# Layer 1's, the pre-attention's and layer 2 routing's steps reordered; the recurrence's weights loaded in layer 0's block; an unread matmul a turn ahead of the attention

## The chip, the core and the metric

One core of a Trainium2 chip runs the whole program in one launch. The metric is the device time of one execution in microseconds (us). The core has five engines that run beside each other and meet only at semaphores: TensorE (PE: matmuls, and PEld: the loading of its stationary operand), VectorE (DVE), ScalarE (ACT), GpSimd (POOL) and SyncE (SP, which issues DMA transfers).

## The reference

The input is x, 64 batches of 128 tokens of 128 features, with an adjacency matrix of 128x128 for each batch. Four layers follow, each a graph part and a feed-forward part, both added to x after a layer norm. Cut to what matters here:

```
x = x + L0_gnn(norm(x), adj)    # relu(adj @ h @ W_rel + h @ W_root), h a second norm of x
x = x + L0_ffn(norm(x))         # recurrence over the 128 tokens: three gates, cell, hidden state; weights U_c U_i U_o V_c V_i V_o, biases b_c b_i b_o
x = x + L1_gnn(norm(x), adj)    # relu((adj @ (x @ W_bot)) / rowsum(adj) + x @ W_top + bias)
x = x + L1_ffn(norm(x))         # router on the mean over the tokens of each batch, top 2 of 8 experts for each batch
x = x + L2_gnn(norm(x), adj)    # attention, 8 heads of 16, softmax times the adjacency
x = x + L2_ffn(norm(x))         # shared expert (128 to 512 to 128) plus top 2 of 8 experts for each token
x = x + L3_gnn(norm(x), adj)
x = x + L3_ffn(norm(x))         # top 1 of 32 experts for each token
```

All of it is in 32-bit floats.

## The kernel before

The 64 batches are taken as 16 groups (NG) of 4 (G), so that a group is a tile of 128 partitions x 512 columns (GW). X, AT (the transposed adjacency), FEAT, AUX and EXP are large buffers in SBUF that the stages use in turn; `PS[0]` to `PS[7]` are the eight banks of PSUM. The program is a row of blocks. In a block each engine has its own instruction stream. Between two blocks all engines meet (`release`, line 97), and the semaphores are cleared.

The order of each stream is written out by hand. `in_turn` and `unrolled` (lines 56 and 65) take a list of pairs (lag, step): in turn j each step is issued for group j - lag, in the order of the list. An engine executes its stream in that order, so a step that waits holds back all steps behind it. `reused(engine, semaphore, i, lag)` (line 70) waits until step i - lag has given its buffer free; with lag 1 a single buffer is shared, with lag 2 there are two that alternate (`par` is i % 2).

The blocks that the change touches:

- Layer 0's graph part (lines 224 to 382). SP loads x and adj for 16 groups (lines 230, 231), two groups ahead, and has nothing else to do.
- The recurrence (from line 385). SP loads the nine weights and three tensors for layer 1 (lines 391 to 396). TensorE and ScalarE wait for the first nine. Each of 128 steps goes through TensorE, ScalarE and VectorE; unread matmuls (line 429) fill TensorE's pauses.
- Layer 1's graph part (lines 477 to 635). TensorE's turn is xT, hidden, project, root, feat, aggregate. `hidden` (line 603) transposes the recurrence's states of group j into PS[0], and VectorE's `add` (line 553) adds them to X and takes the statistics of the sum (lines 172 and 176). GpSimd makes the norm's factors from these (lines 509 to 513). ScalarE normalises (`norm`, line 573), TensorE transposes (`xT`, line 195), ScalarE copies (line 567), TensorE multiplies by the two weights (`project` line 615, `root` line 621) and by the adjacency (`aggregate`, line 633), VectorE adds the root part's bias (`root`, line 531), mixes (`mix`, line 539), adds and takes statistics (`add2`), ScalarE normalises again (`norm2`, line 581), TensorE transposes (`feat`, line 195), and ScalarE copies the result to FEAT, with the sum over each batch's tokens as a by-product of four activations (line 593, `accum_out`). That sum, XM, feeds layer 1's router.
- The pre-attention (lines 894 to 959). VectorE: statistics (`stats`) and the bias of the attention's output (`bias`, line 920). GpSimd: the factors. ScalarE: `norm` (line 931), the copies `xT` (line 937) and `values` (line 941). TensorE: `xT` and `values` (line 955, eight passes).
- Layer 2's routing (lines 1171 to 1447). Each token gets its two experts and a place in a list. GpSimd takes the deviation of group i (`dev`, lines 182 and 184) and sends the rows of group i to DRAM with eight indirect DMAs (`send`, line 1199). VectorE: `stats`, `norm` (line 1388), `top` (lines 1395 to 1404), `choice` (to line 1424), `place` (lines 1429 to 1436), `add` (line 1440). TensorE: `xT` (line 1252), `logits` (line 1259), `rank` (lines 1287 to 1293), and the shared expert's two products, `up` (line 1268, four matmuls of 512 columns) and `down` (line 1276). ScalarE: `xT`, `twin` (a second copy of the rows), `th`, `gelu` (line 1353). Then a table is made from the counts (line 1301 on), and the experts' part follows.

A matmul of 32-bit floats takes two passes, each a record of its own; a transpose takes one.

Of the kernel before, what the change touches and what calls it, by code (L numbers as in the profile page):

```python
# [78 lines left out]
def program(nc, a, out):  # L79
    ctx = ExitStack()  # L80
    with ctx:
# [74 lines left out]
        def column(v):  # L156
            return v.rearrange("(p a) -> p a", a=1)
# [58 lines left out]
        s = sems("l0", "in0 in1 adjT_ps adjT raw mv var pw rstd r2 xn x1 h_ps hT hw_ps hw conv relu back x2 "  # L216
# [6 lines left out]

        with nc.Block() as block:
            @block.sync
            def _(sp):
# [5 lines left out]
                unrolled(NG, [(0, load)])  # L232

# [137 lines left out]
        s = sems("rnn", "zero x_even x_odd g i o gt it ot hc ig c ct h w w1")  # L371
        wr = {}
        for gate in "cio":
            for mat in "UV":
                wr[mat + gate] = lb(f"w_{mat}{gate}", [H, H])
            wr["b" + gate] = lb(f"w_b{gate}", [H, 1])
# [7 lines left out]
        wtop, wbot = EXP[:, 4096:4096 + H], EXP[:, 4096 + H:4096 + 2 * H]  # L384
        b1rows = EXP[:, 4096 + 2 * H:4096 + 3 * H]
        ROWSUM = PS[6][:, 0:B]
        with nc.Block() as block:
            @block.sync
            def _(sp):
                for gate in "cio":  # L390
                    sp.dma_start(wr["U" + gate][:], a["L0_ffn_U_" + gate]).then_inc(s.w, 16)
                    sp.dma_start(wr["V" + gate][:], a["L0_ffn_V_" + gate]).then_inc(s.w, 16)
                    sp.dma_start(wr["b" + gate][:], column(a["L0_ffn_b_" + gate])).then_inc(s.w, 16)
                sp.dma_start(wtop, a["L1_gnn_weight"][0:H, :]).then_inc(s.w1, 16)
                sp.dma_start(wbot, a["L1_gnn_weight"][H:2 * H, :]).then_inc(s.w1, 16)
                sp.dma_start(b1rows, a["L1_gnn_bias"].partition_broadcast(P)).then_inc(s.w1, 16)
                sp.wait_ge(s.w1, 3 * 16)

# [6 lines left out]
            def _(pe):  # L405
                half = STEPS * B // 2

                def inputs(j, par, gate_at, part):

                    gate = "ico"[gate_at]  # L410
                    pe.matmul(PS[2 * gate_at + par][:, part * half:(part + 1) * half], wr["U" + gate][:],
# [3 lines left out]
                def turn(j, par, prefetch):  # L415

                    for u in range(STEPS):
                        step = j * STEPS + u
                        pe.wait_ge(s.h if step else s.zero, step if step else 2)
                        for gate_at, (gate, sem) in enumerate(zip("ico", (s.i, s.g, s.o))):  # L420
                            pe.matmul(PS[2 * gate_at + par][:, u * B:(u + 1) * B], wr["V" + gate][:],  # L421
# [8 lines left out]
                pe.wait_ge(s.w, 9 * 16)  # L430
# [7 lines left out]
            def _(act):  # L438
                def turn(j, par):
                    for u in range(STEPS):  # L440
                        step, sp_ = j * STEPS + u, u % 2
                        for at, (gate, made, done, f) in enumerate((("i", s.i, s.it, ACT.Sigmoid), ("c", s.g, s.gt, ACT.Tanh),
# [3 lines left out]
                                           bias=wr["b" + gate][:]).then_inc(done, 1)  # L446
# [46 lines left out]
        with nc.Block() as block:  # L493
# [1551 lines left out]
```

## Time and profile before

| | us |
|---|---|
| median of three runs | 2015.53 |
| the three runs | 2016.48, 1934.81, 2015.53 |
| the profiled execution, its own time | 1941.87 |
| its span, from the first to the last instruction | 1940.1 |

In the profiled execution the stretches between the meetings of all engines are: layer 0's graph part 0 to 110, the recurrence 110 to 413, layer 1's graph part 413 to 563, its router 563 to 585, its experts 585 to 725, the pre-attention 725 to 786, the attention 786 to 1054, layer 2's routing 1054 to 1261 and its table to 1272, its experts to 1540, layer 3 to the end.

How to read it: times are microseconds from the start of the span. PE is TensorE's matmuls, PEld its weight loads, SPq the queue of SyncE that issues DMAs. L553 is line 553 of the kernel. x8 behind a row says that eight instructions are merged in it. The clock is the granted clock of TensorE, 1.0 for 2.4 GHz and 0.5 for 1.2 GHz, in the mean over a stretch.

### The profile page before, as it was taken

Reading aid. Unit: us, or ns where it says so; the run is one execution under the profiler, and the core shown is the slowest. Engines: PE = TensorE matmul, PEld = TensorE weight load, DVE = VectorE, ACT = ScalarE, POOL = GpSimd, SP = SyncE. Lnnn points to the kernel's source line nnn. Section 1 sums busy time; section 2 is a strip of 40 time slices with the busy share of each in tenths; the row PEclk is TensorE's granted clock in tenths of the full one; section 3 lists DMA queues with packets and bytes.
Section 4 is the critical chain, followed back from the end, with each engine's and each line's share of the span. In section 5 each row is a group of like instructions: output and inputs, shape, how many; then the busy total and the mean of one; then the engine's idle time right before and its main releaser. Section 6 shows DMA issues by size and latency. Waiting matters only on the chain. (4 is left out here: it accounts for less than half of the span.)

```text
span 1940.1 us, 42716 instructions
## 1 busy us (share of the span) xinstructions
PE 1656.8 (85%) x13042; PEld 1362.5 (70%) x13042; DVE 1085.2 (56%) x4176; ACT 951.0 (49%) x2955; POOL 794.2 (41%) x1359
## 2 busy tenths in 40 slices
PE   7968899985649987899997799989999798884995
PEld 5746677765649986788885567789999655563663
DVE  7823333346546775699997645143333377743452
ACT  5844444436556656766664233356666444430000
POOL 6600000013326766111112577736656425543664
PEclk9989999988879995999998589989999899976886
DMA  3200000010004420000002211122222342105331
GB/s 112 66 13 2 1 1 1 1 25 1 1 20 130 125 85 1 2 3 2 3 3 71 81 48 50 52 65 71 71 73 71 87 114 72 48 29 107 92 86 32
DMA packets 129697, 92.87 MB, mean 48 GB/s; under 512 B 25166, under 2 KB 120305, under 8 KB 129476
## 3 DMA queue, kind: packets, MB, share of 16 engines
q1 hardware_dynamic: 108276, 61.46, 11.8%
q0 software_dynamic: 13568, 25.90, 4.1%
q10 hardware_dynamic: 7632, 2.79, 0.8%
q8 instruction: 112, 1.84, 0.4%
q14 instruction: 109, 0.89, 0.2%
HBM read 58.81 MB, written 33.35 MB: 48 GB/s over the span
## 5 line engine op out<-in xcount | busy, mean ns | idle before, releaser
L1207 POOL DMA_INDIRECT scratch_made<-FEAT x136 | 154.6, 1137 | 121.9 <-DVE FEAT L1496 119.1
L1365 ACT ACTIVATE FEAT<-BANKS,EXP 128x128 f32<-128x128 f32 x544 | 155.0, 368 | 82.7 <-PE BANKS L1318 82.7
L1060 ACT ACTIVATE EXP<-BANKS,NEGMAX 128x128 f32<-128x128 f32 x512 | 139.0, 382 | 59.3 <-DVE NEGMAX L1072 58.0
L1318 PE MATMUL BANKS<-FEAT 128*128 128x128 f32 x1088 | 145.4, 277 | 0.0
L1327 PE MATMUL BANKS<-AUX,FEAT 128*128 x1088 | 144.2, 276 | 0.4 <-ACT FEAT L1365 0.4
L1199 POOL DMA_INDIRECT scratch_sent<-FEAT,POS x128 | 123.7, 967 | 38.9 <-issue 37.8
L1318 PEld LDWEIGHTS BANKS<-FEAT 128*128 128x128 f32 x1088 | 133.9, 194 | 0.0
L1327 PEld LDWEIGHTS BANKS<-AUX,FEAT 128*128 128x128 f32 x1088 | 132.9, 193 | 0.6 <-issue 0.6
L509 POOL TENSOR_SCALAR NEG<-MV 128x4 f32<-128x4 f32 x16 | 3.6, 228 | 310.4 <-DVE MV L176 310.4
L989 POOL COPY EXP<-AUX 128x32 f32<-128x32 f32 x256 | 42.1, 209 | 215.8 <-PE BANKS L1035 215.8
L429 PE MATMUL BANKS<-FEAT,ident 128*128 128x256 f32 x460 | 126.8, 393 | 0.0
L1625 POOL DMA_INDIRECT out_x<-FEAT x96 | 93.9, 979 | 74.5 <-DVE FEAT L2012 46.6
L1496 DVE TENSOR_TENSOR FEAT<-BANKS,B2BC 128x128 f32<-128x128 f32 x136 | 39.5, 290 | 136.8 <-PE BANKS L1327 136.8
L464 DVE TENSOR_TENSOR ig<-gates 128x64 f32<-128x64 f32 x128 | 28.7, 224 | 119.0 <-ACT gates L445 119.0
L445 ACT ACTIVATE gates<-BANKS,w_bi 128x64 f32<-128x64 f32 x128 | 40.3, 315 | 108.7 <-PE BANKS L421 108.7
L1844 ACT ACTIVATE FEAT<-BANKS,EXP 128x128 f32<-128x128 f32 x24 | 8.8, 367 | 172.8 <-PE BANKS L1787 172.8
L1072 DVE TENSOR_REDUCE NEGMAX<-BANKS 128x4 f32<-128x512 f32 x128 | 82.5, 686 | 19.0 <-PE BANKS L1011 16.4
L850 ACT ACTIVATE WF<-BANKS,BT 128x128 f32<-128x128 f32 x256 | 73.0, 368 | 40.0 <-PE BANKS L824 40.0
L421 PEld LDWEIGHTS BANKS<-AUX,w_Vi 128*128 128x128 f32 x256 | 38.2, 188 | 71.0 <-DVE AUX L470 70.9
L429 PEld LDWEIGHTS BANKS<-FEAT,ident 128*128 128x128 f32 x460 | 80.8, 191 | 7.4
L1081 DVE SCALAR_TENSOR_TENSOR EXP<-AT,BANKS 128x512 f32<-128x512 f32 x128 | 81.7, 679 | 0.0
L1617 POOL DMA_INDIRECT scratch_sent<-FEAT,POS x64 | 63.6, 993 | 36.6 <-DVE POS L1935 21.3
(385 smaller groups left out, 4538.2 us busy)
## 6 DMA issues: line engine op xcount, KB each, us to landing
EXP<-in_L_ffn_W SPq DMA_DIRECT2D x128, 128.0 KB, 2.1
FEAT<-scratch_sent SPq DMA_DIRECT2D x136, 64.5 KB
EXP<-scratch_made SPq DMA_DIRECT2D x32, 256.0 KB, 3.3
FEAT<-scratch_sent SPq DMA_DIRECT2D x96, 65.5 KB, 1.9
X<-in_x SPq DMA_DIRECT2D x16, 256.0 KB, 2.9
STAGE<-in_adj SPq DMA_DIRECT2D x16, 256.0 KB, 3.3
scratch_sent<-NONE SPq DMA_DIRECT2D x48, 65.5 KB, 3.2
scratch_sent<-FEAT,POS POOLq DMA_INDIRECT x192, 2.3
```

The costliest lines, as they stand in the source:

```text
L429: pe.matmul(PS[7][:, 0:half], ident[:], cols(FEAT, j, STEPS * B, 0, half), start=True, stop=True)
L850: last = act.activation(tile(HB[:, i % 2], k * C1 + c), tile(PS[i % 2], k * C1 + c), ACT.Gelu, bias=BT1[:, c, 2 * i + k:2 * i + k + 1])
L1060: last = act.activation(tile(EXS[:, par], 4 * k + n), tile(PS[j], c), ACT.Exp, bias=NEGMAX[:, par, 4 * k + n:4 * k + n + 1])
L1072: v.tensor_reduce(NEGMAX[:, par, 4 * k:4 * k + 4].rearrange("p (j c) -> p j c", j=2), BANKS[:, 2 * k:2 * k + 2, 0:NC * T].rearrange("p j ( ...
L1081: v.scalar_tensor_tensor(PTA[:, par, 4 * k * T:4 * (k + 1) * T].rearrange("p (n t) -> p n t", n=4), adj, ADJ_EPS, PS[4 + k].rearrange("p ( ...
L1199: pool.indirect_dma_start(out=sent2, out_offset=bass.IndirectOffsetOnAxis(ap=POS[:, n, b:b + 1], axis=0), in_=OUTBOX[:, i % R_SEND, n, k, ...
L1207: pool.indirect_dma_start(out=made2, out_offset=bass.IndirectOffsetOnAxis(ap=XI_I[:, t % R_IN, H:ROW2], axis=0), in_=YO[:, t % R_OUT, :], ...
L1318: last = pe.matmul(tile(PS[2 + t % 2], c), W1R[:, t % R_W, c * P:(c + 1) * P], XTI[:, t % 3, :], start=True, stop=True)
L1327: last = pe.matmul(PS[4 + t % 2][:, 0:H], tile(HR[:, t % R_H], c), W2_2.rearrange("p c d -> p (c d)")[:, bass.ds(e * F2 + c * H, H)], star ...
L1365: last = act.activation(tile(HR[:, t % R_H], c), tile(PS[2 + t % 2], c), ACT.Gelu, bias=BT[:, c, t:t + 1])
L1617: pool.indirect_dma_start(out=sent3, out_offset=bass.IndirectOffsetOnAxis(ap=POS3[:, b:b + 1], axis=0), in_=OUTBOX3[:, i % R_SEND3, k, :], ...
L1625: pool.indirect_dma_start(out=out_rows, out_offset=bass.IndirectOffsetOnAxis(ap=XI3_I[:, t % R3, H + 2:ROW3], axis=0), in_=YO3[:, t % R3, ...
```

## The change

- The twelve loads of the recurrence's block go to the end of SP's stream in layer 0's block. The weights get their place in EXP (columns 0 to 770), which is free then. The waits for them go, since the block's end waits for them.
- Layer 1: `hidden` uses two banks, PS[0] and PS[7], and stands behind `root` in TensorE's turn. The sums over the tokens are made on TensorE, by four matmuls of one column each ahead of `feat`'s transposes, into the bank that held the adjacency's row sums. ScalarE copies FEAT in one instruction, and XM once at the end.
- Pre-attention: the copy of the values goes from ScalarE to VectorE, with lag 3. TensorE gets a matmul of 512 columns into PS[7], which nobody reads, between `values` and `xT`.
- Routing: new lags and orders on all four engines. The waits for the constants move from the streams' start to their first use.

```diff
+                for gate in "cio":
+                    sp.dma_start(wr["U" + gate], a["L0_ffn_U_" + gate]).then_inc(s.later, 16)
+                    sp.dma_start(wr["V" + gate], a["L0_ffn_V_" + gate]).then_inc(s.later, 16)
+                    sp.dma_start(wr["b" + gate], column(a["L0_ffn_b_" + gate])).then_inc(s.later, 16)
+                sp.dma_start(wtop, a["L1_gnn_weight"][0:H, :]).then_inc(s.later, 16)
+                sp.dma_start(wbot, a["L1_gnn_weight"][H:2 * H, :]).then_inc(s.later, 16)
+                sp.dma_start(b1rows, a["L1_gnn_bias"].partition_broadcast(P)).then_inc(s.later, 16)
+                sp.wait_ge(s.later, 12 * 16)
...
-                pe.wait_ge(s.w, 9 * 16)
-                act.wait_ge(s.w, 9 * 16)
...
-                    v.tensor_tensor(cols(X, i), cols(X, i), PS[0], ALU.add).then_inc(s.x1, 1)
+                    v.tensor_tensor(cols(X, i), cols(X, i), PS[7 * par], ALU.add).then_inc(s.x1, 1)
...
-                    for k in range(G):
-                        last = act.activation(cols(FEAT, i, GW, k * T, T), tile(PS[1], k), ACT.Copy,
-                                              accum_out=cols(XM, i, G, k, 1))
-                    last.then_inc(s.feat, 1)
+                    act.copy(cols(FEAT, i), PS[1]).then_inc(s.feat, 1)
                 unrolled(NG, [(3, xT), (2, norm), (5, norm2), (3, xw), (5, feat)])
+                act.copy(XM[:], ROWSUM)
...
-                    reused(pe, s.x1, i, 1)
+                    reused(pe, s.x1, i, 2)
-                        last = pe.transpose(tile(PS[0], k), HS_v[:, G * i + k, :], ident[:])
+                        last = pe.transpose(tile(PS[7 * par], k), HS_v[:, G * i + k, :], ident[:])
...
                     reused(pe, s.feat, i, 1)
+                    if i == 0:
+                        pe.wait_ge(s.sum, 1)
+                    for k in range(G):
+                        pe.matmul(ROWSUM[:, G * i + k:G * i + k + 1], tile(WE[:, par], k), ones[:, 0:1], start=True, stop=True)
                     transpose4(pe, PS[1], WE[:, par], s.y_ps)
...
-                unrolled(NG, [(3, xT), (0, hidden), (3, project), (3, root), (5, feat), (3, aggregate)])
+                unrolled(NG, [(3, xT), (3, project), (3, root), (0, hidden), (5, feat), (3, aggregate)])
...
-                unrolled(NG, [(0, stats), (2, bias)])
+                def values(i, par, half):
+                    v.wait_ge(s.v_ps, i + 1)
+                    v.tensor_copy(cols(VAL, i), PS[2 + par]).then_inc(s.v, 1)
+                unrolled(NG, [(0, stats), (2, bias), (3, values)])
...
-                unrolled(NG, [(1, xT), (0, norm), (2, values)])
+                unrolled(NG, [(1, xT), (0, norm)])
...
+                def keep_warm(i, par, half):
+                    pe.matmul(PS[7].rearrange("p (g h) -> p g h", g=G), ident[:], ident[:].unsqueeze(1).to_broadcast([P, G, H]),
+                              start=True, stop=True)
-                unrolled(NG, [(2, values), (1, xT)])
+                unrolled(NG, [(2, values), (0, keep_warm), (1, xT)])
...
-                in_turn(NG, [(0, dev), (6, send)])
+                in_turn(NG, [(0, dev), (4, send)])
...
-                in_turn(NG, [(1, xT), (2, logits), (5, rank), (8, up), (9, down)])
+                in_turn(NG, [(1, xT), (7, up), (1, logits), (3, rank), (8, down)])
...
-                in_turn(NG, [(1, xT), (2, twin), (3, th), (8, gelu)])
+                in_turn(NG, [(1, xT), (1, twin), (2, th), (7, gelu)])
...
-                in_turn(NG, [(1, norm), (0, stats), (3, top), (6, place), (4, choice), (10, add)])
+                in_turn(NG, [(0, stats), (1, norm), (4, place), (2, top), (3, choice), (9, add)])
```

## Rows read from the trace of the kernel before

**Rows 1.** Stretches: length; busy of PE, PEld, DVE, ACT, POOL; clock; DMA share; GB/s
```profile
413.00:563.00 150.00, 88.76 (x578) 82.88 (x578) 90.17 (x371) 86.97 (x289) 52.16 (x129) 0.85 0.04 9
725.00:786.00 61.00, 42.87 (x192) 36.22 (x192) 30.01 (x145) 41.78 (x96) 32.88 (x64) 0.59 0.00 1
```

**Rows 2.** Timeline, recurrence's opening: start, us, engine, line, operation [idle before]
```profile
76.11 0.51 SPq L231 DMA_DIRECT2D STAGE<-in_adj  x1
...
109.91 0.34 SPq L391 DMA_DIRECT2D w_Uc<-in_L_ffn_U_c  x1
...
115.79 2.07 PE L411 MATMUL BANKS<-FEAT,w_Ui 128*128 128x256 f32 x4 [7.82 <-DMA w_bo<-in_L_ffn_b_o]
```

**Rows 3.** Waits in layer 1: who waited for whom, us in total, times, longest
```profile
PE BANKS L603 <- DVE X L553: 45.3, 14, 3.6
```

**Rows 4.** Timeline of one turn of layer 1
```profile
506.73 0.69 DVE L531 TENSOR_TENSOR WF<-BANKS,EXP 128x512 f32<-128x512 f32 x1 [1.27 <-PE BANKS L621]
...
507.86 0.60 PE L195 MATMUL BANKS<-ident,WA 128*128 128x128 f32 x4
...
508.06 1.13 DVE L539 SCALAR_TENSOR_TENSOR WD<-BANKS,INV,WF 128x128 f32<-128x128 f32 x4 [0.64 <-PE BANKS L633]
...
508.97 1.65 ACT L573 ACTIVATE WA<-X,NMR,RS 128x128 f32<-128x128 f32 x4
...
510.52 1.64 ACT L581 ACTIVATE WE<-X,NMR,RSB 128x128 f32<-128x128 f32 x4
...
513.10 0.38 DVE L176 BATCH_NORM_AGGREGATE MV<-STATS 128x2 f32<-128x6 f32 x4
...
515.22 0.20 POOL L513 TENSOR_TENSOR NMR<-NEG,RS 128x4 f32<-128x4 f32 x1
```

**Rows 5.** TensorE's timeline in layer 1: xT of turns 4, 16 and 17
```profile
425.80 0.60 PE L195 MATMUL BANKS<-ident,WA 128*128 128x128 f32 x4
...
535.17 0.60 PE L195 MATMUL BANKS<-ident,WA 128*128 128x128 f32 x4
...
540.99 0.60 PE L195 MATMUL BANKS<-ident,WA 128*128 128x128 f32 x4
```

**Rows 6.** TensorE's timeline, routing: eight passes of eight columns, high clock
```profile
1200.59 0.96 PE L1259 MATMUL BANKS<-wr,WD 128*128 128x8 f32 x8
```

**Rows 7.** TensorE's timeline in the pre-attention: first and last xT, and values
```profile
730.38 1.08 PE L195 MATMUL BANKS<-ident,WA 128*128 128x128 f32 x4 [9.65 <-ACT WA L931]
...
753.78 2.08 PE L955 MATMUL BANKS<-EXP,FEAT 128*128 128x128 f32 x8 [0.68 <-ACT FEAT L937]
...
778.30 1.16 PE L955 MATMUL BANKS<-EXP,FEAT 128*128 128x128 f32 x8 [0.68 <-ACT FEAT L937]
...
782.72 0.66 PE L195 MATMUL BANKS<-ident,WA 128*128 128x128 f32 x4 [0.39 <-ACT WA L931]
```

**Rows 8.** Chain that ended last: layer 3's unread matmul of 512 columns
```profile
1559.57 0.86 PE BANKS L1687 x2
```

**Rows 9.** GpSimd's timeline, routing: first send, deviations 7 and 15, last send
```profile
1084.86 1.26 POOL L1199 DMA_INDIRECT scratch_sent<-FEAT,POS  x1 [1.12 <-DVE POS L1436]
...
1094.97 0.21 POOL L182 TENSOR_TENSOR RS<-MV,epsilon 128x4 f32<-128x4 f32 x1
...
1186.55 0.21 POOL L182 TENSOR_TENSOR RS<-MV,epsilon 128x4 f32<-128x4 f32 x1
...
1257.61 0.96 POOL L1199 DMA_INDIRECT scratch_sent<-FEAT,POS  x1 [0.30 <-issue]
```

**Rows 10.** TensorE's timeline, routing: xT 15, two ups, the table's first matmul
```profile
1190.89 0.60 PE L1252 MATMUL BANKS<-ident,FEAT 128*128 128x128 f32 x4
...
1234.96 3.85 PE L1268 MATMUL BANKS<-WB,WC 128*128 128x512 f32 x8
...
1242.22 3.85 PE L1268 MATMUL BANKS<-WD,WC 128*128 128x512 f32 x8
...
1260.30 0.29 PE L1301 MATMUL BANKS<-CAR,ones 128*128 128x8 f32 x2
```

More of the change, by code:

```diff
@@ L213, in program @@
         W = weights
-        s = sems("l0", "in0 in1 adjT_ps adjT raw mv var pw rstd r2 xn x1 h_ps hT hw_ps hw conv relu back x2 "
+        s = sems("l0", "later in0 in1 adjT_ps adjT raw mv var pw rstd r2 xn x1 h_ps hT hw_ps hw conv relu back x2 "
                        "raw2 mv2 var2 rstd2 n2 m2 xn2 x_ps xT")
@@ L222, in program @@
         NEG = sb("NEG", [P, 2, G])
+        wr = {}
+        for at, gate in enumerate("cio"):
+            wr["U" + gate], wr["V" + gate] = (tile(EXP, 2 * at + k) for k in range(2))
+            wr["b" + gate] = EXP[:, 6 * H + at:6 * H + at + 1]
+        wtop, wbot = EXP[:, 4096:4096 + H], EXP[:, 4096 + H:4096 + 2 * H]
+        b1rows = EXP[:, 4096 + 2 * H:4096 + 3 * H]
         with nc.Block() as block:
@@ L370, in program @@
         layer()
[L371 to L376, printed above, removed]
+        s = sems("rnn", "zero x_even x_odd g i o gt it ot hc ig c ct h")
         HS = AUX
@@ L383, in program @@
         NT = T // STEPS
-        wtop, wbot = EXP[:, 4096:4096 + H], EXP[:, 4096 + H:4096 + 2 * H]
-        b1rows = EXP[:, 4096 + 2 * H:4096 + 3 * H]
         ROWSUM = PS[6][:, 0:B]
         with nc.Block() as block:
[L388 to L397, printed above, removed]
             @block.gpsimd
@@ L410, in inputs @@
                     gate = "ico"[gate_at]
-                    pe.matmul(PS[2 * gate_at + par][:, part * half:(part + 1) * half], wr["U" + gate][:],
+                    pe.matmul(PS[2 * gate_at + par][:, part * half:(part + 1) * half], wr["U" + gate],
                               cols(FEAT, j, STEPS * B, part * half, half), start=(part == 0), stop=False,
@@ L420, in turn @@
                         for gate_at, (gate, sem) in enumerate(zip("ico", (s.i, s.g, s.o))):
-                            pe.matmul(PS[2 * gate_at + par][:, u * B:(u + 1) * B], wr["V" + gate][:],
+                            pe.matmul(PS[2 * gate_at + par][:, u * B:(u + 1) * B], wr["V" + gate],
                                       cols(HS, j, STEPS * B, u * B, B), start=False, stop=True,
@@ L445, in turn @@
                             act.activation(gates[:, at, sp_, :], PS[2 * at + par][:, u * B:(u + 1) * B], f,
-                                           bias=wr["b" + gate][:]).then_inc(done, 1)
+                                           bias=wr["b" + gate]).then_inc(done, 1)
                         act.wait_ge(s.c, step + 1)
                         act.activation(tanhc[:, sp_, :], cell[:, sp_, :], ACT.Tanh).then_inc(s.ct, 1)
-                act.wait_ge(s.w, 9 * 16)
                 for j in range(NT):
@@ L937, in xT @@
                     act.copy(cols(FEAT, i), PS[par]).then_inc(s.xT, 1)
-                def values(i, par, half):
-                    act.wait_ge(s.v_ps, i + 1)
-                    act.copy(cols(VAL, i), PS[2 + par]).then_inc(s.v, 1)
-                unrolled(NG, [(1, xT), (0, norm), (2, values)])
+                unrolled(NG, [(1, xT), (0, norm)])
             @block.tensor
@@ L1282, in rank @@
                     pe.wait_ge(s.m, i + 1)
+                    if i == 0:
+                        pe.wait_ge(s.ctab, 4)
                     if i:
@@ L1295, in _ @@
                 pe.wait_ge(s.w, 16)
-                pe.wait_ge(s.ctab, 4)
-                in_turn(NG, [(1, xT), (2, logits), (5, rank), (8, up), (9, down)])
+                in_turn(NG, [(1, xT), (7, up), (1, logits), (3, rank), (8, down)])
                 pe.wait_ge(s.car, NG)
@@ L1382, in norm @@
                     slot, par = i % R_SEND, i % 2
+                    if i == 0:
+                        v.wait_ge(s.ctab, 4)
                     v.wait_ge(s.rstd, i + 1)
```

1 line of the change is left out of this document (removed).

## The prediction

> **What bounds the kernel now.** I read the table of stretches first, cut at the places where every engine stands still between two blocks, then the waits of the stretches that the change touches, then the order of instructions inside one turn of each. The edits touch four stretches: the weights of the recurrence, layer 1's graph step, the pre-attention, and layer 2's routing. The rest of the program (attention, both expert parts, layer 3) is not edited. In the table the reader is to see that TensorE is busy for 88.8 of layer 1's 150 us, at a granted clock of 0.85, and for 42.9 of the pre-attention's 61 us, at 0.59 [rows 1]: chains of waits between engines, partly at TensorE's low level. In the routing two engines run without a gap, GpSimd until 1258.6 and TensorE until 1260.3 [rows 9, 10].
>
> **The weights.** The recurrence's first matmul stands at 115.79 and had waited for the last of nine loads, the first of which was issued at 109.91, when the block opened [rows 2]. The last load of layer 0 is issued at 76.11, and SP has nothing to do after it until 109.91; the twelve moved loads take 12 x 0.45 = 5.4 us to issue and end some 24 us before the block does, so they cost nothing there. TensorE can then start about where SP did: 5.8 us less. TensorE starts behind a wait of 7.8 us now and of 2 us then; if its low clock lasted a step longer or shorter, that would be 1 us. Bounds: 4.8 to 6.3 us gained. I take 5.8.
>
> **Layer 1.** Of all waits of this stretch the largest on TensorE is that of the hidden-state transposes (line 603) for VectorE's addition (line 553): 45.3 us in 14 waits, 3.6 us each [rows 3]. PS[0] is one bank, so group j's transposes wait until group j-1 was added, and that addition stands on VectorE behind the previous group's mix, addition and statistics. Everything later in TensorE's turn stands behind it: project, root, feat, aggregate. From the first to the last full turn twelve turns take 535.17 - 425.80 = 109.4 us, 9.11 each [rows 5].
> With two banks, and the transposes moved behind the root product, this wait goes. What is late next? In one turn [rows 4]: xT at 507.86, the copy, then norm at 508.97 (1.11 later), norm2 at 510.52, its end at 512.16 (4.30 after xT). Only then can feat start. To it the change adds eight passes of one-column matmuls ahead of the transposes. The nearest row is the eight passes with eight columns, 0.96 us [rows 6]; as neighbours overlap a little I take 0.85, between 0.5 and 1.0. Then four transposes (0.45 to the next issue, of 0.60 busy) and the aggregate (0.95 of 1.1 busy). Sum: 4.30 + 0.05 + 0.85 + 0.45 + 0.95 = 6.6 us a turn. VectorE: from mix at 508.06 to the end of the second statistics at 513.48 is 5.4, and root's addition of 0.7 (line 531) makes 6.1, just under it. GpSimd has the factor of the next norm at 515.42, 7.56 after xT; norm wants it at 6.6 + 1.11 = 7.7, so that is just in time too. ScalarE gets four activations with their sum readings replaced by one copy of 0.6, off this path. Gain: 12 x (9.11 - 6.6) = 30 us.
> Given back: the three turns after the last hidden group never had this wait, and each now carries the row sums, 3 x 0.9; the last feat gets them at the low clock, 1.8, and XM's copy, 0.3, against 0.7 saved on ScalarE. About 4 us. Net 26 us. Bounds: 31 if the row sums are cheap and all turns run at the high clock; 12 if the clock falls every second turn as it does now.
> The Trainium skill, "TensorE: Matmul & The Clock Gate", section "Back-to-back issue gap", gives matmuls of 1 to 64 columns a spacing of about 60 cycles, 25 ns, so the eight passes would take 0.2 us and a turn would fall to VectorE's 6.1; by it the sum would be some 7 us better, 1901. The row of 0.96 us for eight passes speaks against it [rows 6], and I go by the row.
>
> **The pre-attention.** The values' copy goes from ScalarE to VectorE. At the high clock a turn is norm (1.65, as in layer 1 [rows 4]), TensorE's transposes (0.7), the copy (0.5) and the next norm, 2.9 us. The values' copy lies beside the transposes, so moving it gains nothing by itself. VectorE has 30.0 us of work in the stretch [rows 1], 1.9 a turn, and the copy adds the 0.7 of an operation of that size out of PSUM (line 531 [rows 4]): 2.6 and gaps, still under the turn. The unread matmul takes 0.86 us at the high clock [rows 8] and stands between values and xT; 0.9 + 0.86 exceed norm's 1.65, so a turn becomes 3.1 us there. At the low clock eight passes take 2.08 instead of 1.16 [rows 7], and a turn becomes 1.75 (values) + 1.7 (unread) + 1.1 (xT) + 0.6 (copy) = 5.1. The gain must come from leaving the low clock early: a mean of 0.59 between levels of 0.5 and 1.0 is about four fifths of the stretch low. The first two unread matmuls fall in TensorE's idle time ahead of the first xT and cost nothing. Now 15 turns take 782.72 - 730.38 = 52.3 us. With two turns low and thirteen high: 10.2 + 40.3 = 50.5. Gain 2 us. Bounds: 6 gained with no low turn, 24 lost if all are low.
>
> **The routing.** It looks as if it must gain: sends start at lag 4 instead of 6 and the expert products' lags fall by one. First send now at 1084.86, six and a half turns after 1054: 4.7 a turn. Two turns less, and the constants' wait moved from the statistics to the first norm (1.4), put it at 1074. From there GpSimd is the bound and never waits: eight sends and one deviation pair take (1186.55 - 1094.97) / 8 = 11.45 us [rows 9]. But deviation i stands on GpSimd's in-order queue behind send i-5 now, where it stood behind i-7. Deviation 15 had 16-7 = 9 groups of sends ahead of it; it will have 11. So it comes at 1074 + 10.1 + 10 x 11.45 = 1198.6 instead of 1186.55. VectorE's norm 15 and TensorE's transposes of it follow 2.5 us later, 1201.1 instead of 1190.89 [rows 10] (they were 1.8 late for other reasons): 10.2 later. From there TensorE is full until 1260.30. By the new lags it has one up and one down less behind that point (1242.22 - 1234.96 = 7.26 together), two ranks (1.25 each) and one logits (0.8): 10.6 less. Up now waits once a turn for a gelu behind ScalarE's th, +0.5. Sum 0: sends end at 1250 instead of 1258.6, and nobody waits for them, because TensorE ends at 1260 as before. Bounds: 3 gained to 5 lost (start of the sends off by 2; turns longer than 11.45 at the low clock).
>
> **The sum.** 5.8 + 26 + 2 + 0 = 34 us. The profiled execution took 1941.87 us (span 1940.1 and 1.8 around it): 1908 us, 1.8% less. The three timed runs lie on two levels, 1934.81 alone and 2015.53 with 2016.48; the profiled one is near the lower. None of my terms knows which level a run takes. On the upper one the same 34 us give 1982. I give the lower as the time and let the range hold both.
>
> **The rivals.**
> A, the clock does not hold. Place: layer 1 and the pre-attention, whose added matmuls are paid double when the clock is low. For it: means of 0.85 and 0.59 with TensorE 59% and 70% busy [rows 1]. Against it: TensorE's long waits in layer 1 are the 3.6 us ones that go, and the first turn without one, 535.17 to 540.99, took 5.8 us with all its matmuls at the high clock (transposes 0.60) [rows 5]. If it is low throughout, a layer 1 turn is 1.8 + 1.7 + 1.7 + 0.9 + 1.8 + 0.9 + 1.7 = 10.5, 12 x 1.4 + 11 for the tail = 28 lost; the pre-attention loses 24; with the weights +46: 1988 us, slower than before by 2.4%. The gain is gone once two fifths of these turns are low, and 2% are lost at nine tenths. Chance 0.04.
> B, partly so: some turns of layer 1 low, or TensorE later in the routing's turns than deviation 15: 10 to 20 us less gain, 1918 to 1928. Chance 0.22.
> C, more: one-column matmuls at half my price, pre-attention high from its first turn, sends early enough: 40 to 50 us gain, 1892 to 1902. For it: VectorE's 6.1 a turn allows it, and the stretches behind may start in a better phase. Chance 0.24.
> D, the change is hidden: layer 1's wait returns as a wait of feat for norm2 of the same length. VectorE then would be at 9 us a turn, against its 6.1. 1935, chance 0.02.
> My own case, 1902 to 1918: 0.48.
>
> **How the numbers follow.** A difference under 2%, 39 us, is about what measuring this kernel can tell from none. On one level, faster by more than that is C, 0.24, and slower is A, 0.05 with what I overlook. But the median before stands on the upper level; should the median after stand on the lower, it will read as faster whatever the mechanism. I give that a bit more than one in three of the rest: 0.26. Faster 0.50, slower 0.05, within 0.45. Range: C's lower end, 1892, to B and my case on the upper level, 1990; left out are the best of C and part of A and B on the upper level, under 0.2. My case alone on the lower level is 1902 to 1918.
>
> **What would show it.** First matmul of the recurrence at 110; no wait of line 603 for 553; layer 1 turns of 6.6 us with granted clock near 1.0 and the stretch near 124 us; pre-attention turns of 3.1 us, clock over 0.9; first send some 20 us after the routing opens, the last 176 us later, and TensorE full until some 206 us after the opening. Wrong would be: a layer 1 turn over 8 us, a clock under 0.9 in either stretch, or a routing shorter than 200 us.

## The result, and the profile after

| | before | after |
|---|---|---|
| timed executions, us | 2016.48, 1934.81, 2015.53, 1940.26 | 1909.43, 1906.1, 1913.84, 1908.29 |
| median of the four | 1977.89 | 1908.86 |
| profiled execution, us | 1941.87 | 1909.43 |
| its span, mean clock | 1940.1, 0.909 | 1907.7, 0.930 |

The ratio of after to before is 0.984 with an interval of 0.981 to 0.987: 1.6% less, within the 2% that count as no change. It leaves out the two executions before near 2015 us; why these stand apart is the first finding below. None of the four executions after is on that level.

The two profiled executions differ by 32.4 us in span. Read at the meetings of all engines, the gain builds up like this:

| up to | before | after | gained so far |
|---|---|---|---|
| layer 1's graph part opens | 413.64 | 407.61 | 6.0 |
| it ends | 562.4 | 533.6 | 28.8 |
| pre-attention, first xT | 730.38 | 700.85 | 29.5 |
| attention, first matmul | 786.64 | 756.28 | 30.4 |
| attention, last addition | 1053.29 | 1024.86 | 28.4 |
| routing, matmul of the table | 1260.30 | 1231.59 | 28.7 |
| layer 2's experts, first matmul | 1271.74 | 1242.97 | 28.8 |
| end | 1940.1 | 1907.7 | 32.4 |

The stretches answer to [rows 1] (same columns):

```profile
407.60:533.60 126.00, 94.51 (x704) 86.75 (x705) 88.96 (x370) 76.58 (x178) 52.19 (x129) 0.92 0.04 11
700.00:756.00 56.00, 42.47 (x220) 29.35 (x220) 36.45 (x142) 33.46 (x79) 30.52 (x58) 0.90 0.00 1
```

Clock: 0.92 where it was 0.85, 0.90 where it was 0.59. The recurrence's opening, ScalarE's and TensorE's timeline, answers to [rows 2]:

```profile
110.45 1.28 ACT L440 ACT_TABLE_LOAD   x1 [0.90 <-PEq L101]
```

```profile
110.49 4.75 PE L407 MATMUL BANKS<-FEAT,EXP 128*128 128x256 f32 x12 [1.98 <-PEq L101]
115.08 0.78 PE L417 MATMUL BANKS<-AUX,EXP 128*128 128x64 f32 x6
...
117.25 0.43 PE L417 MATMUL BANKS<-AUX,EXP 128*128 128x64 f32 x2 [0.25 <-DVE AUX L464]
```

The first matmul stands at 110.49. What I had not looked for: ScalarE's table load now stands beside the U products, so TensorE waits 0.25 us before its second step. In the kernel before, the load came behind the first V matmuls and TensorE waited 1.57 us:

```profile
121.02 1.28 ACT L445 ACT_TABLE_LOAD   x1 [12.00 <-PE BANKS L421]
```

```profile
120.60 0.33 PE L421 MATMUL BANKS<-AUX,w_Vi 128*128 128x64 f32 x2
...
124.09 0.43 PE L421 MATMUL BANKS<-AUX,w_Vi 128*128 128x64 f32 x2 [1.57 <-DVE AUX L470]
```

Layer 1's largest wait on TensorE [rows 3] is gone; the largest now is that of the row sums for norm2 (who waited for whom, us in total, times, longest):

```profile
PE BANKS L622 <- ACT WE L575: 14.6, 15, 3.6
```

One turn of layer 1 after, against [rows 4]; all lines are from one timeline:

```profile
455.00 0.60 PE L195 MATMUL BANKS<-ident,WA 128*128 128x128 f32 x4
...
457.68 1.65 ACT L575 ACTIVATE WE<-X,NMR,RSB 128x128 f32<-128x128 f32 x4
458.17 0.74 PE L595 MATMUL BANKS<-ident,AUX 128*128 128x128 f32 x4
...
458.52 0.65 DVE L547 TENSOR_TENSOR X<-X,BANKS 128x512 f32<-128x512 f32 x1
...
459.38 1.05 PE L622 MATMUL BANKS<-ones,WE 128*128 128x1 f32 x8 [0.47 <-ACT WE L575]
...
460.29 0.64 PE L195 MATMUL BANKS<-ident,WE 128*128 128x128 f32 x4
...
460.76 1.06 PE L629 MATMUL BANKS<-WC,AT 128*128 128x128 f32 x8
...
461.66 0.60 PE L195 MATMUL BANKS<-ident,WA 128*128 128x128 f32 x4
```

norm2 ends 4.33 us after xT (forecast 4.30), the row sums take 0.91 to the next issue (0.85), feat 0.47, aggregate 0.90: a turn is 6.66 us (forecast 6.6). The xT of turns 4 and 16, against [rows 5]:

```profile
421.95 0.60 PE L195 MATMUL BANKS<-ident,WA 128*128 128x128 f32 x4
...
501.59 0.60 PE L195 MATMUL BANKS<-ident,WA 128*128 128x128 f32 x4
```

79.64 us for twelve turns instead of 109.4. TensorE in the pre-attention, against [rows 7, 8] (L956 is the unread matmul, two passes a turn):

```profile
700.85 1.12 PE L195 MATMUL BANKS<-ident,WA 128*128 128x128 f32 x4 [1.24 <-ACT WA L931]
...
709.83 1.91 PE L956 MATMUL BANKS<-ident 128*128 128x512 f32 x2
...
713.91 1.02 PE L956 MATMUL BANKS<-ident 128*128 128x512 f32 x2
...
752.04 0.66 PE L195 MATMUL BANKS<-ident,WA 128*128 128x128 f32 x4 [0.39 <-ACT WA L931]
```

Two turns at the low clock (5.4 and 5.3 us), then 3.13 us each; 15 turns in 51.2 us against 52.3. Routing, GpSimd's timeline (first send, deviation 15, last send) and TensorE's (xT of group 15, the table's first matmul), against [rows 9, 10]:

```profile
1045.01 1.26 POOL L1200 DMA_INDIRECT scratch_sent<-FEAT,POS  x1 [2.04 <-DVE POS L1440]
...
1169.68 0.21 POOL L182 TENSOR_TENSOR RS<-MV,epsilon 128x4 f32<-128x4 f32 x1
...
1220.61 0.96 POOL L1200 DMA_INDIRECT scratch_sent<-FEAT,POS  x1 [0.30 <-issue]
```

```profile
1172.32 0.66 PE L1253 MATMUL BANKS<-ident,FEAT 128*128 128x128 f32 x4 [1.36 <-DVE FEAT L1392]
...
1231.59 0.29 PE L1303 MATMUL BANKS<-CAR,ones 128*128 128x8 f32 x2
```

From the attention's last addition (1053.29 before, 1024.86 after): first send 31.6 before, 20.2 after; deviation 15 133.3 and 144.8; table 207.0 and 206.7.

### The profile page after: what moved, and what is told of

Read it like the earlier page. It is cut to its first block and busy times, and to the rows that moved or that the text cites. A ratio compares the mean times of both kernels' runs of the same rounds, so it can differ in the third digit from the quotient of the medians.

```text
span 1907.7 us, 42926 instructions
## 1 busy us (share of the span) xinstructions
PE 1657.1 (87%) x13202; PEld 1355.8 (71%) x13202; DVE 1096.7 (57%) x4192; ACT 934.4 (49%) x2828; POOL 794.3 (42%) x1359
## 5 line engine op out<-in xcount | busy, mean ns | idle before, releaser
L440 ACT ACTIVATE gates<-BANKS,EXP 128x64 f32<-128x64 f32 x384 | 97.5, 315 | 112.7 <-PE BANKS L417 112.7
L417 PEld LDWEIGHTS BANKS<-AUX,EXP 128*128 128x128 f32 x768 | 95.4, 191 | 70.5 <-DVE AUX L464 70.4
L1200 POOL DMA_INDIRECT scratch_sent<-FEAT,POS x128 | 124.1, 970 | 39.6 <-issue 37.5
L417 PE MATMUL BANKS<-AUX,EXP 128*128 128x64 f32 x768 | 112.7, 283 | 19.4 <-DVE AUX L464 17.0
L1073 DVE TENSOR_REDUCE NEGMAX<-BANKS 128x4 f32<-128x512 f32 x128 | 82.6, 686 | 18.5 <-PE BANKS L1012 11.5
L458 DVE TENSOR_TENSOR ig<-gates 128x64 f32<-128x64 f32 x128 | 28.8, 225 | 111.7 <-ACT gates L440 111.7
```

The source lines that it names most:

```text
L440: act.activation(gates[:, at, sp_, :], PS[2 * at + par][:, u * B:(u + 1) * B], f, bias=wr["b" + gate]).then_inc(done, 1)
L1073: v.tensor_reduce(NEGMAX[:, par, 4 * k:4 * k + 4].rearrange("p (j c) -> p j c", j=2), BANKS[:, 2 * k:2 * k + 2, 0:NC * T].rearrange("p j ( ...
L1200: pool.indirect_dma_start(out=sent2, out_offset=bass.IndirectOffsetOnAxis(ap=POS[:, n, b:b + 1], axis=0), in_=OUTBOX[:, i % R_SEND, n, k, ...
```

## The experiments

Each kernel is told against the one that its edit starts from. "Low recurrence" is an execution in which the recurrence ran partly at TensorE's low clock, as c1 shows: its mean clock is 0.832 to 0.872, and its time some 75 us above that of the others in the same batch.

**c1, the kernel before once more** (no edit).

> The kernel before once more, so that its two levels of time (1935 to 1940 and 2015 to 2016 us) can be read beside the granted clock of each execution. Theory 1: the upper level is a lower granted clock of TensorE over the whole span; an execution near 2015 us then shows a mean clock well under the 0.909 of the profiled one (under 0.87), and the change, whose own stretches ran at 0.85 and 0.59, does not remove it. Theory 2: the upper level is a stall of 75 us in one place that has nothing to do with TensorE's clock; then the clock of such an execution is within 0.01 of 0.909 times the ratio of the spans.

Of six executions four stood at 2008 to 2018 us with a mean clock of 0.860 to 0.866, two at 1930 to 1931 with 0.922. The profiled one took 2014.76. Its window 126 to 256, and the same window of the kernel before (columns as in [rows 1]):

```profile
126.00:256.00 130.00, 130.00 (x458) 116.33 (x459) 34.28 (x153) 45.52 (x152) 0.00 (x0) 0.50 0.00 1
```

```profile
126.00:256.00 130.00, 115.92 (x689) 90.01 (x688) 51.64 (x230) 57.98 (x228) 0.00 (x0) 1.00 0.00 1
```

The whole of the difference lies in the recurrence: layer 1 opens at 489.0 instead of 413.6, 75 us later, and the span is 73 us longer. Theory 1 has the right cause, a low granted clock, but not over the whole span: it is in one place. TensorE's timeline at the start and at the end of the low stretch:

```profile
122.27 0.43 PE L421 MATMUL BANKS<-AUX,w_Vi 128*128 128x64 f32 x2
...
125.87 0.69 PE L421 MATMUL BANKS<-AUX,w_Vi 128*128 128x64 f32 x2 [1.58 <-DVE AUX L470]
...
344.63 0.33 PE L421 MATMUL BANKS<-AUX,w_Vi 128*128 128x64 f32 x2
```

The first step's V matmuls are at the high clock already (0.43); then comes the pause of 1.58 us, and behind it they take 0.69. The clock is low until about 343, the first step without a matmul of the adjacency's row sums, though TensorE has no gap. This is the only trace of a low execution; the others are told by their mean clock and time.

Not every execution with the pause falls, and why one does is not shown. One thing differs in the traces that were kept, the time of the clock's rise. In c1 the U products of the third gate, four passes, were low to their end; with the same pause behind them and no fall they took 1.40 us (before), 1.43 (c3), 1.57 (c4) and 1.78 (c5), so the clock had risen earlier. In c9, which has no pause, they were as late as in c1, and the clock stayed high. c1, then c9:

```profile
120.56 1.91 PE L411 MATMUL BANKS<-FEAT,w_Uo 128*128 128x256 f32 x4
```

```profile
120.44 1.91 PE L411 MATMUL BANKS<-FEAT,w_Uo 128*128 128x256 f32 x4
```

**c2, the weights' loads alone; c3, layer 1's part alone; c4, the routing's part alone** (each the hunks of that part on the kernel before).

> Only the twelve loads moved into layer 0's block. Forecast term 5.8 us: first matmul of the recurrence near 110 instead of 115.79, layer 1's graph part opens 6 us earlier, everything behind it unchanged in length: 1930 to 1936 us on the lower level. Rival: layer 0 or the recurrence's first steps give it back; then layer 1 opens within 2 us of where it did.

> Only layer 1's part (two banks, hidden behind root, row sums on TensorE). The kernel with all parts shows turns of 6.66 us and a stretch of 126 instead of 148.8 us. If the part stands by itself: the stretch is 124 to 128 us here too, and the total 1914 to 1920 us on the lower level. Rival: part of those 23 us came from the recurrence starting 6 us earlier (another phase of the clock at layer 1's opening); then the stretch here is above 130 us.

> Only layer 2's routing part (new lags). Theory (forecast): first send 10 to 12 us earlier, deviation 15 about 12 us later from the opening, TensorE's last matmul of the stretch 206 to 208 us after the opening as before: total 1934 to 1942 us on the lower level, a difference of 0 to 1 us in the routing. Rival: the earlier start carries through and the routing ends 8 to 12 us earlier, 1925 to 1932 us.

c2: four executions, 1929.72 to 1943.07 (ratio 0.9986, 0.9939 to 1.0033), none low; its total can't be told from the kernel before's. Its table load stands at 110.25 already. Layer 1 opens at 406.5, 7.1 us earlier; from there to its last xT it takes 137.7 us against 133.8, so this execution gave 4 us back, at a granted clock of 0.71 from 413 to 463 against 0.80. c3: 1913.52 to 1920.79 and one low one at 1991.11 (ratio 0.990, 0.985 to 0.995). Its turns are 6.64 us and opening to last xT is 108.5 us, as in the kernel after (108.9): the part stands by itself. c4: 1925.86, 1931.4 and two low ones (ratio 0.995, 0.989 to 1.002). GpSimd and TensorE of c4, deviation 15 and the table's first matmul:

```profile
1195.00 0.21 POOL L182 TENSOR_TENSOR RS<-MV,epsilon 128x4 f32<-128x4 f32 x1
```

```profile
1256.91 0.29 PE L1302 MATMUL BANKS<-CAR,ones 128*128 128x8 f32 x2
```

With the attention's last addition at 1050.46 these are 144.5 and 206.5 us, the first send 20.1: earlier by 11, later by 11, and at the end 0.6 less. Its total of 1925.86 to 1931.4 looks like the rival's, but the routing was not shorter; see the spread below.

**c5, one tanh early.** On the kernel before:

```diff
+                act.activation(tanhc[:, 1, 0:1], ones[:, 0:1], ACT.Tanh)
                 act.wait_ge(s.w, 9 * 16)
```

> The kernel before with one more activation of one column (tanh of a constant) at the start of ScalarE's stream in the recurrence, so that the activation table is loaded while the weights are awaited and not behind the first V matmuls. TensorE's wait of 7.8 us for the weights stays; its pause of 1.57 us after the first step becomes 0.25. So far the executions with the weights' loads in this block stood near 2010 us 12 times in 29 (recurrence at a clock of 0.62), those with the loads moved 0 times in 8. Theory 1: what lets the recurrence fall to the low clock is the pause of 1.57 us just as the clock has risen; then none of the six executions here is near 2010 us, all 1925 to 1945. Theory 2: it is the wait of 7.8 us ahead of it, or the place of the weights; then 2 or 3 of 6 are near 2010.

A miss: the tanh ran without a table load (at 110.37), the load of 1.28 us still stood at the first gate, a sigmoid, and the pause was still 1.57 us. So it is one more kernel with the pause: one of six executions low (2018.16), the others 1935 to 1950.

**c6, the pause put back into the kernel after.**

```diff
+                pool.wait_ge(s.i, 1)
+                pool.tensor_tensor(scr[:], epsilon[:], mhalf[:], ALU.pow).then_inc(s.late, 1)
...
+                            if step == 0 and at == 0:
+                                act.wait_ge(s.late, 1)
                             act.wait_ge(made, step + 1)
```

> The kernel after with the pause put back: ScalarE's first gate waits for one GpSimd operation of 1.04 us that itself waits for the first V matmul, so that TensorE stands about 1.5 us after the first step. Weights stay in layer 0's block. Theory 1: 1 to 3 of the six executions show the recurrence at the low clock, 75 us longer (1980 to 1990 us); the others 1907 to 1915. Theory 2: all six lie at 1906 to 1916.

Two of five executions low, 1983.95 and 1989.26, the others 1907 to 1912. ScalarE's and TensorE's timelines:

```profile
115.70 1.28 ACT L445 ACT_TABLE_LOAD   x1 [6.14 <-PE BANKS L420]
```

```profile
118.78 0.88 PE L420 MATMUL BANKS<-AUX,EXP 128*128 128x64 f32 x6 [1.58 <-DVE AUX L469]
```

The added wait moved the table load behind it as well, so that the pause is the same 1.58 us as before. The weights had been there all along and TensorE's wait ahead of the block was 1.98, so neither their place nor a long wait for them is needed. Pause and late load always come together in these runs: that the pause acts, and not the load itself, is argued and not shown.

**c9, one sigmoid early.** On the kernel before, c5's line with `ACT.Sigmoid`.

> The kernel before with one sigmoid of one column at the start of ScalarE's stream in the recurrence (the tanh of the run before didn't fetch the table that the gates need: its load of 1.28 us still stood behind the first V matmuls, TensorE paused 1.57 us, and one of six executions was near 2010 us). Now the load should stand beside TensorE's wait of 7.8 us for the weights, which stays, and the pause after the first step should be 0.25 us. So far 18 of 52 executions with the pause had the recurrence at the low clock, 0 of 16 without. Theory 1 (the pause decides): none of six is near 2010 us. Theory 2 (the wait of 7.8 us is enough by itself): 2 of 6 are.

(The counts at that point were 18 of 51; 52 is a slip.) None of six was low: 2019 to 2032 us, while of the eleven executions of the kernel before in that batch seven were (2101 to 2112; the others 2013 to 2034; every kernel took some 85 us longer in that batch, as told at the end). ScalarE and TensorE:

```profile
111.05 1.28 ACT L449 ACT_TABLE_LOAD   x1 [0.90 <-PEq L101]
```

```profile
124.49 0.43 PE L421 MATMUL BANKS<-AUX,w_Vi 128*128 128x64 f32 x2 [0.30 <-DVE AUX L471]
```

TensorE's wait for the weights is still 7.77 us here. So that wait is not enough to bring the fall, and without the pause and the late load there is none. Over all runs: with the pause 30 of 80 executions were low (the kernel before 20 of 55, c1 4 of 6, c3 1 of 4, c4 2 of 4, c5 1 of 6, c6 2 of 5), without it none of 48.

**c7, no unread matmul** in the pre-attention of the kernel after.

```diff
-                unrolled(NG, [(2, values), (0, keep_warm), (1, xT)])
+                unrolled(NG, [(2, values), (1, xT)])
```

> The kernel after without the unread matmul in the pre-attention (the values' copy stays on VectorE). Turns there took 3.13 us with it at the high clock, 5.35 at the low one; without it the kernel before took 2.87 at the high and 3.61 at the low clock. Theory (forecast): the unread matmul buys the high clock early; without it the clock rises anywhere between turn 2 and turn 12 and the 15 turns take 44 to 52 us, against 51.2: total between 3 us more and 6 us less than the kernel after. Rival: the copy on VectorE alone shortens a low turn (ScalarE has 0.7 us less), then low turns are under 3.4 us.

1896.65 to 1911.74. First and last xT:

```profile
701.19 1.09 PE L195 MATMUL BANKS<-ident,WA 128*128 128x128 f32 x4 [9.64 <-ACT WA L931]
...
754.26 0.66 PE L195 MATMUL BANKS<-ident,WA 128*128 128x128 f32 x4 [0.39 <-ACT WA L931]
```

53.1 us, low until the last two turns, 3.61 us each. The rival is out: the copy on VectorE doesn't shorten a low turn. Without unread matmuls the clock rises at a varying time: the 15 turns took 52.3 (before), 44.3, 45.8, 51.6, 47.2, 44.3, 51.6 (c1 to c5, c9) and here 53.1 us, 48.8 in the mean. With one in every turn they took 51.2 (after), 51.1, 49.4, 51.3, 49.3 and 51.2 (c6, c8, c10, c11, c13), 50.6 in the mean. The second group lies closer together; that its mean is worse isn't clear of the first one's spread.

**c8, the deviations ahead** in the routing of the kernel after.

```diff
-                in_turn(NG, [(0, dev), (4, send)])
+                for k in range(5):
+                    dev(k)
+                for k in range(NG):
+                    send(k)
+                    for d in ((5, 6), (7, 8))[k] if k < 2 else (k + 7,):
+                        if d < NG:
+                            dev(d)
```

> The kernel after, routing: GpSimd takes the deviations as early as the seven places of the send ring allow, deviation i+7 right behind the sends of group i, instead of deviation i+5. My step: deviation 15 behind the queue of sends holds TensorE's last third. If right: deviation 15 comes behind 9 groups of sends instead of 11, at 20 + 9 x 11.45 = 123 us after the opening instead of 145; TensorE's products end at 183 to 190 instead of 206.7; then the sends (end at 196) set the experts' start, which comes at 198 to 203 instead of 218 after the opening: 15 to 20 us less in all, near 1892. Rival: TensorE's own work or VectorE holds its end; then TensorE's end stays within 3 us of 206 and nothing is gained.

1890.82 to 1903.43, ratio to before 0.978 (0.974 to 0.981). GpSimd, then TensorE (table, experts' first matmul):

```profile
1149.32 0.22 POOL L182 TENSOR_TENSOR RS<-MV,epsilon 128x4 f32<-128x4 f32 x1
```

```profile
1211.48 0.29 PE L1309 MATMUL BANKS<-CAR,ones 128*128 128x8 f32 x2
...
1226.02 0.45 PE L1319 MATMUL BANKS<-ident,FEAT 128*128 128x128 f32 x1 [4.64 <-DMA FEAT<-scratch_sent]
```

From the last addition at 1024.83: 124.5, 186.7 and 201.2 us, against 144.8, 206.7 and 218.1 after. The deviation's place in GpSimd's queue set TensorE's end, and now the sends do (last one at 1220.96).

**c10, the token sums back on ScalarE** (layer 1 of the kernel after: `feat` on ScalarE as before the change, no row sums on TensorE).

> The kernel after, layer 1: the sums over the tokens again as a by-product of four activations on ScalarE, no row sums on TensorE; two banks and the new order stay. Theory (my step): norm2's end, eight one-column passes of 0.91 us, feat and aggregate make the turn of 6.66 us, so without the row sums it falls to VectorE's 6.0 to 6.1: layer 1's stretch 119 to 121 us instead of 126. Rival: ScalarE, with 0.7 us more in each turn, then sets it; turns stay at 6.6 to 7.0 and the row sums cost nothing.

Its batch is one of two in which every kernel took 80 to 95 us longer, all of it behind the routing's opening (below), so only the stretches ahead of that are read. xT of two turns:

```profile
441.15 0.60 PE L195 MATMUL BANKS<-ident,WA 128*128 128x128 f32 x4
...
446.98 0.60 PE L195 MATMUL BANKS<-ident,WA 128*128 128x128 f32 x4
```

Turns of 5.8 to 6.5, 6.2 us in the mean; opening to last xT 101.1 us against 108.9, and layer 1's stretch 116 us against 126 (119 to 121 expected). The row sums on TensorE, instead of on ScalarE, cost 8 to 10 us.

**c11, one bank** (`hidden` behind `root`, but into PS[0] alone).

> The kernel after, layer 1: hidden stands behind root as it does there, but uses one bank, PS[0], again. In the kernel after, hidden starts 3.17 us after xT and VectorE's addition of the group before ends 4.17 us after xT. Theory: the move does most of the work and the second bank little; hidden waits 1.0 us more, of which about 0.5 was idle time ahead of the row sums anyway, so a turn becomes 6.9 to 7.2 us and the stretch 130 to 133. Rival: the second bank is what took the wait away; the turn goes back to 8 to 9.1 us.

```profile
446.13 0.85 PE L595 MATMUL BANKS<-ident,AUX 128*128 128x128 f32 x4 [0.89 <-DVE X L547]
```

TensorE waits 0.89 us there; turns are 7.09 us (two of 7.5 and 8.3), opening to last xT 113.4 us. Of the 2.45 us that a turn fell, the place gives 2.0 (with the row sums already paid) and the second bank 0.43.

**c12, three edits on the kernel after**: c8's; the unread matmul for the first four groups only; and unread matmuls behind `hidden` in layer 1's first three turns.

```diff
+                    if i >= 4:
+                        return
...
+                def fill(i, par, half):
+                    for _ in range((1, 1, 2)[i] if i < 3 else 0):
+                        pe.matmul(PS[3].rearrange("p (g h) -> p g h", g=G), ident[:],
+                                  ident[:].unsqueeze(1).to_broadcast([P, G, H]), start=True, stop=True)
+                unrolled(NG, [(3, xT), (3, project), (3, root), (0, hidden), (0, fill), (5, feat), (3, aggregate)])
```

> Three edits on the kernel after: deviations ahead in the routing (as in the run with that name, 16.9 us less there); the unread matmul only in the pre-attention's first four turns; and in layer 1's first three turns one, one and two unread matmuls of 512 columns behind hidden, where TensorE stood idle for 4.18 us and the clock had fallen. Expected: layer 1's turn from the first to the second xT falls from 7.6 to about 4.7 us (3 us less), if the clock was kept high by the unread ones; rival: it has fallen anyway, they cost 2 to 3 us. Pre-attention: the high clock stays once reached, turns of 2.87 instead of 3.13 us (3 us less); rival: it falls again, turns of 3.61. Total near 1887 us, between 1882 and 1895.

The pre-attention took 45.5 us: the high clock stayed once reached, turns of 2.87. In layer 1:

```profile
410.10 1.88 PE L633 MATMUL BANKS<-ident 128*128 128x512 f32 x4
...
413.34 0.66 PE L195 MATMUL BANKS<-ident,WA 128*128 128x128 f32 x4 [1.35 <-ACT WA L567]
```

The unread ones ran at the high clock (1.88 for four passes), yet the turns from the first xT on took 6.25, 4.64, 9.35 and 7.11 us, much as without them in c8 (6.61, 4.64, 9.43, 7.10): opening to last xT 108.7 us, nothing gained. A total couldn't be read in this batch.

**c13, the kernel after once more; c14, the three best edits together** (c8's, c10's, and the unread matmul for four groups).

> The kernel after once more, beside the next one on the same chip. On a chip like that of the first calls: 1905 to 1915 us, the recurrence at the high clock in all four executions (theory 1: no pause after the first step, no low recurrence; 0 of 34 so far, against 25 of 62 with the pause). Theory 2 (the absence was chance): one or two of four are 75 us longer.

> The kernel after with three edits: deviations ahead in the routing (16.9 us less in its own run), the token sums back on ScalarE (layer 1's stretch 116 us instead of 126 in its own run), the unread matmul only in the first four turns of the pre-attention (45.5 us instead of 49.4 to 51.2 there). If they add up: 30 us less than the kernel after, 1880 us, and no execution with a low recurrence. Rival: a stage behind takes some back by an earlier fall of the clock; 1885 to 1892 us.

Both fell into the second long batch (before: 2025 to 2041, low ones 2100 to 2105). c13: 2004 to 2015, no low one of four. c14 reached the attention's last addition at 1010.5 against c13's 1024.0: 13.5 us less; behind that nothing can be read.

**c15, c14's kernel again.**

> The combined kernel of c14 once more. In c9 to c14 every kernel, the one before too, took 80 to 95 us longer than in the first calls, all of it behind the opening of layer 2's routing, where engines stood for up to 20 us with no work to wait for. If this run meets the earlier conditions (kernel before at 1930 to 1945 us), it should stand near 1880 us (16.9 from the deviations ahead and 13.5 from the other two edits, under the 1909 of the kernel after), by the rival 1885 to 1892. If it doesn't, the first 1012 us repeat c14's and the rest stays unread.

The kernel before at 1930 to 1940 and two low ones; c15 1881.42 in the median, 1876.88 to 1890.28, none low. Ratio 0.971, 0.968 to 0.975. Last addition at 1008.3, table 186.5 us later, experts 201.0: the gains add up. This version beats both kernels, the one after by 27 us in the medians of two batches (0.971 of the kernel before against 0.984).

## Why the prediction was right and where it failed

**The failed step is the one on the level**, in "the sum" and "how the numbers follow": "None of my terms knows which level a run takes." One of them does. I set a time of the lower level, 1908, beside a median of the upper one, 2015.53, so the forecast read as 5.3% less; on equal terms I had forecast 1.8%, and 1.6% was measured. And I held that the change might read as faster "whatever the mechanism", by chance. The runs show a mechanism: with the weights moved, ScalarE's wait for them went, its table load came to stand beside the U products, the pause of 1.57 us in TensorE's second step is gone, and with it every low recurrence (0 of 48 against 30 of 80, and put back by c6). I had read TensorE's opening up to the first matmul [rows 2], not up to the second step, and I looked for 1 us of clock there, where 75 were at stake. The range's upper end, 1990, covered an upper level that the changed kernel doesn't have.

**The time itself**, 1908 against 1908.86, was in part luck. Layer 1 gave 3 us less than forecast, the attention took 2 back, and 3.6 us less behind the routing, which the change doesn't explain, made up for them.

**Weights**: 5.8 forecast, 6.0 measured to layer 1's opening; 7.1 in c2.

**Layer 1**: 26 forecast, 22.8 in the pair of profiles. Against all profiles with the old layer 1 (133.8 to 138.7 us from opening to last xT, six of them, mean 136.4) and the new (108.5 to 109.1, six, mean 108.9) it is 27.5. The turn was 6.66 against 6.6, bound by norm2, row sums, feat, aggregate as worked out; the stretch was 126 us at a clock of 0.92, against 124 and near 1.0. What I had not in the sum is the start: a turn of 7.6 at the low clock and one of 8.4, in which TensorE waits 2.25 us for the first norm2. The row sums cost 0.91 each turn. The table in the Trainium skill, "TensorE: Matmul & The Clock Gate", section "Back-to-back issue gap", taken for the eight passes gave 0.2; the section calls it the isolated gap of a single matmul, which leaves out the weight load, and here each pass loads its own weights: the trace has 0.91. The turn of about 6.1 that the 0.2 led to came only when the row sums were taken out (c10).

**Pre-attention**: 2 forecast, 1.1 in the pair's 15 turns (0.8 by the attention's opening), and the attention began at the low clock and gave 1.9 back. Turns were as forecast (two low, then 3.13). But the base was one draw of 52.3 out of 44.3 to 53.1: by the means above an unread matmul in every turn gains nothing and may lose 2 us. Taking its cost in thirteen high turns as the price of reaching them was the weak point; four of them do (45.5, 48.3 and 45.3 us in c12, c14, c15).

**Routing**: 0 forecast, 0.3 measured. Deviation 15 came 11.5 us later from the opening (forecast 12), xT 15 came 9.9 later (10.2), TensorE's end as before; c4 alone repeats it and c8 shows the cause.

**The rest**, not edited: 0 forecast. 0.7 less in layer 1's router and experts and 3.6 less behind the routing. That isn't the change: from the experts' first matmul to TensorE's last, kernels that are equal there took 638.6 to 648.3 us (c1 to c4, before, after).

**The rivals**: A, the clock doesn't hold: excluded, 0.92 and 0.90. B and C are not what happened in the total. D: the wait that came back is 0.47 us in a full turn before the row sums, not 3.6.

## What to carry to other kernels

When runs fall on two levels, find out before anything else which stretch makes them: one profile of an execution on the upper level is worth more than a sum of parts. Then look at each short pause of TensorE near a rise of its clock, and at what late one-time work (here a table load on another engine, kept late by one more wait ahead of it) makes it. A cost taken from one execution in a stretch whose clock flips at a varying time needs several executions as its base. And on an in-order queue, count what stands ahead of the last item, not when the first one leaves.

## What the runs showed of the hardware that I had not expected

- A pause of 1.58 us just behind the clock's rise was followed in c1 by some 220 us at the low clock (0.50 from 126 to 256) with no gap on TensorE. The Trainium skill says, in "TensorE: Matmul & The Clock Gate", section "What's actually happening", that "the default state is throttled, and activity releases the throttle"; this trace has activity without release. Why it ended near 343, where the adjacency's row sums of one column end, is open, as is why most executions with the pause don't fall: one profile shows a fall, and no run varied its end or the time of the rise.
- A table load is 1.28 us, as the Trainium skill has it ("ScalarE: Activation LUTs", section "What ACT_TABLE_LOAD costs"). The 1.38 us of draining that it adds there don't show: the pause was 1.57 us with the load and 0.25 without. And a tanh needed no load where the first sigmoid did (c5, c9). Where the load stands went by the waits ahead of the first gate: with only the wait for its V matmul it ran ahead of that wait (110.45 after, 110.25 in c2); with a second wait, for the weights before (121.02) or for GpSimd in c6 (115.70), it stood behind both. So it is the dropped wait that moved the load; no run keeps the wait with the weights moved.
- In the batches of c9 to c12 and of c13 and c14 the same kernels took 80 to 95 us longer, all behind the routing's opening. Engines stood there with nothing of the kernel to wait for: the view names no engine of the core but "remote", which the kernel after doesn't show in this stretch. One of c13's waits in the routing (who, for whom, us in total, times, longest):

```profile
DVE RB L1433 <- remote: 47.4, 9, 8.1
```

One of these batches was on the chip on which c5 to c8 had run without it, so it is not that chip alone. The cause wasn't found.
